# Shared-key attention on Trainium2: diagonal blocks masked by GpSimd on the exponentials in place of a mask product on TensorE

## The reference

```
q = (x @ Wq).reshape(B, T, 16, 16);  k = x @ Wk;  v = x @ Wv          # k, v: T x 16
scores = einsum('bihd,bjd->bhij', q, k) / sqrt(16)
scores = where(j <= i, scores, -inf)
out = einsum('bhij,bjd->bihd', softmax(scores), v) @ Wo + bo
```

## Time and profile before

| | us |
|---|---|
| median of 3 runs | 1820.72 (1815.22 to 1824.67) |
| the profiled execution | 1815.07 |
| its span | 1813.3 |
| TensorE busy | 1660.7 (92%) |
| VectorE busy | 1010.2 (56%) |
| ScalarE busy | 760.0 (42%) |
| GpSimd busy | 386.1 (21%) |
| score, mask and value products of the stage, busy | 205.3, 54.3, 150.0 |

### The profile page before, as it was taken

One profiled execution on the slowest core, in us unless ns is written; L12 is line 12 of the kernel. 1 busy time (PEld: TensorE's weight loads), 2 busy tenths in 40 slices (PEclk: granted clock), 3 DMA queues, 4 the chain that ended last, 5 costly groups with the idle time before them and its releaser, 6 DMA issues.

```text
span 1813.3 us, 25325 instructions
## 1 busy us (share of the span) xinstructions
PE 1660.7 (92%) x9852; PEld 985.2 (54%) x9852; DVE 1010.2 (56%) x1735; ACT 760.0 (42%) x1757; POOL 386.1 (21%) x457
## 2 busy tenths in 40 slices
PE   7999789999999999699997888968999999979998
PEld 4666444433333344445563555745677777764556
DVE  4665677777787753534435743325676666731222
ACT  3421346667667766131101121136666666632110
POOL 2321000001000000400000076514444443530000
PEclk9998889999999999699998999989999999999999
DMA  5000120000000002010000030000000020000000
GB/s 171 2 7 18 52 71 2 2 1 2 1 1 2 1 1 98 0 48 0 1 1 15 1 116 1 0 6 1 7 1 7 1 80 1 1 0 1 12 12 23
DMA packets 28360, 34.96 MB, mean 19 GB/s; under 512 B 5713, under 2 KB 24722, under 8 KB 27730
## 3 DMA queue, kind: packets, MB, share of 16 engines
q1 hardware_dynamic: 28242, 33.35, 5.8%
HBM read 23.74 MB, written 2.10 MB: 14 GB/s over the span
## 4 chain that ended last, share of the span: by engine, by line
PE 74%; DVE 13%; POOL 6%; issue 3%; ACT 3%; DMA 0%; SPq 0%; POOLq 0%; DVEq 0%; ACTq 0%
PE PS L1155 7%; PE PS L1142 6%; PE PS L1114 6%; PE PS L1396 6%; PE PS L1402 6%; PE PS L1417 5%; PE PS L2235 3%; DVE arena L1320 3%; PE PS L2224 2%; PE PS L1898 2%; PE PS L2202 2%; PE PS L1881 2%; PE PS L339 2%; POOL arena L2420 2%; PE PS L2177 2%
## 5 line engine op out<-in xcount | busy, mean ns | idle before, releaser
L1244 ACT ACTIVATE arena<-PS 128x512 f32<-128x512 f32 (+3 forms) x640 | 319.7, 534 | 174.3 <-PE PS L1142 77.7
L1320 DVE TENSOR_REDUCE arena<-PS 128x1 f32<-128x1024 f32 (+7 forms) x320 | 329.7, 1061 | 96.1 <-PE PS L1116 68.3
L1142 PE MATMUL PS<-arena 99*128 99x512 bf16 (+3 forms) x640 | 205.3, 352 | 1.4 <-ACT arena L1244 1.0
L1114 PE MATMUL PS<-arena 96*128 96x512 bf16 (+3 forms) x640 | 178.4, 357 | 18.3 <-DVE arena L1320 17.5
L190 POOL TENSOR_TENSOR rstd<-ve,mhalf 128x4 f32<-128x4 f32 x32 | 32.3, 1009 | 606.3 <-DVE ve L218 606.3
L1155 PE MATMUL PS<-arena 128*32 128x512 f32 (+3 forms) x1280 | 150.0, 541 | 2.8 <-ACT arena L1250 1.7
L185 ACT ACTIVATE XT<-PS 128x1024 f32<-128x1024 f32 x32 | 32.8, 1024 | 283.2 <-PE PS L178 283.2
L1142 PEld LDWEIGHTS PS<-arena 99*128 99x128 bf16 x640 | 60.5, 99 | 147.1 <-ACT arena L1244 115.5
L1396 PE MATMUL PS<-XT,arena 128*128 128x512 f32 x256 | 122.7, 602 | 5.6 <-DVE R L200 3.5
L2235 PE MATMUL PS<-arena 128*128 128x256 f32 x512 | 121.0, 379 | 2.0 <-DVE R L200 2.0
L1402 PE MATMUL PS<-XT,arena 128*128 128x512 f32 x256 | 120.3, 592 | 0.0
(11 more groups left out here) (241 smaller groups left out, 2832.4 us busy)
## 6 DMA issues: line engine op xcount, KB each, us to landing
arena<-arena SPq DMA_DIRECT2D x55, 128.0 KB, 2.4
XT<-in_L_attn_xT SPq DMA_DIRECT2D x4, 512.0 KB, 6.9
X<-in_L_attn_x SPq DMA_DIRECT2D x4, 512.0 KB, 9.2
arena<-in_L_attn_out_w SPq DMA_DIRECT2D x1, 2048.0 KB, 7.3
out<-X SPq DMA_DIRECT2D x4, 512.0 KB, 2.9
arena<-in_dmask SPq DMA_DIRECT2D x1, 1024.0 KB, 5.6
arena<-in_L_ffn_W_up SPq DMA_DIRECT2D x1, 1024.0 KB, 5.2
arena<-in_L_ffn_W_gate SPq DMA_DIRECT2D x1, 1024.0 KB, 7.3
```

Source lines behind the costliest of these rows:

```text
L1114: last = pe.matmul(flat[:, o:o + w], q, a.KS[0:SROWS, CH * kc:CH * kc + w], start=True, stop=kc < c)
L1142: last = pe.matmul(PS[:, b, lo:CH], a.KS[0:rows, P * j:P * (j + 1)], a.QS[0:rows, G1 * g + r, CH * c + lo:CH * (c + 1)], start=True, stop= ...
L1244: act.activation(a.PB[:, n % 3, r, lo:CH], PS[:, 4 + x % 3, lo:CH], ACT.Exp, scale=D0 ** -0.5).then_inc(a.e2, 1)
L1320: dve.tensor_reduce(dst, src, AX.X, ALU.max, negate=True).then_inc(a.m1, 1)
```

## The change

The mask of 0 and -1e30 in bf16 and the mask product on diagonal blocks are gone. The exponentials of a diagonal block are computed without a mask, and GpSimd then writes zero where the key is ahead of the query, in the triangle's 128 columns of all four heads, with one `affine_select` of 4 x 128 columns in place. A new semaphore `kept` counts these; `value` waits for it on diagonal blocks. `value(n)` runs in step n+1 in place of step n, and the copy of the sum, the sums, the spread and the inverse move one step with it. GpSimd's new work for block n+1 stands at step n, between `parts` and `spread`.

```diff
@@ Plan1.__init__ @@
-        self.steps = range(-AHEAD1, self.nb + 4)
+        self.steps = range(-AHEAD1, self.nb + 5)
@@
             if i < NI1 - 2:
-                self.den_at[self.first[i + 1] + 1] = i
-            self.rdt_at[self.first[i + 1] + 3] = i
-        self.den_at[self.nb] = NI1 - 2
-        self.den_at[self.nb + 1] = NI1 - 1
-        self.rdt_at[self.nb + 2] = self.rdt_at.pop(self.first[NI1 - 1] + 3)
+                self.den_at[self.first[i + 1] + 2] = i
+            self.rdt_at[self.first[i + 1] + 4] = i
+        self.den_at[self.nb + 1] = NI1 - 2
+        self.den_at[self.nb + 2] = NI1 - 1
+        self.rdt_at[self.nb + 3] = self.rdt_at.pop(self.first[NI1 - 1] + 4)
+        self.masked = {}
+        for n, (i, j, lo) in enumerate(self.blocks):
+            if j >= TPC * (i // 4):
+                self.masked[n] = len(self.masked)
@@ l1_set @@
-    pool.tensor_copy(a.mkb, a.mk).then_inc(a.z, 1)
@@ l1_pe: score @@
         last = pe.matmul(PS[:, b, lo:CH], a.KS[0:rows, P * j:P * (j + 1)], a.QS[0:rows, G1 * g + r, CH * c + lo:CH * (c + 1)],
-                         start=True, stop=j < TPC * c)
-        if j >= TPC * c:
-            last = pe.matmul(PS[:, b, lo:lo + P], k.identb[:, :], a.mkb, start=False, stop=True)
+                         start=True, stop=True)
@@ l1_pe: value @@
-        pe.wait_ge(a.e2, G1 * (n + 1))
+        if n in P1.masked:
+            pe.wait_ge(a.kept, P1.masked[n] + 1)
+        else:
+            pe.wait_ge(a.e2, G1 * (n + 1))
@@ l1_pe: the loop over steps @@
-        if 0 <= n < P1.nb:
-            value(n)
+        if 0 <= n - 1 < P1.nb:
+            value(n - 1)
@@ l1_act: the loop over steps @@
-        if n + 1 in P1.first[1:]:
-            values_out(P1.first.index(n + 1) - 1)
+        if n in P1.first[1:]:
+            values_out(P1.first.index(n) - 1)
@@ l1_pool @@
+    def keep(n):
+        lo = P1.blocks[n][2]
+        p = a.PB[:, n % 3, :, lo:lo + P]
+        pool.wait_ge(a.e2, G1 * (n + 1))
+        pool.affine_select(p, p, pattern=[[0, G1], [1, P]], compare_op=ALU.is_ge, fill=0.0, base=0, channel_multiplier=-1).then_inc(a.kept, 1)
+
     for n in P1.steps:
         if n in P1.mt_at:
             parts(P1.mt_at[n])
+        if n + 1 in P1.masked:
+            keep(n + 1)
         if n in P1.den_at:
             spread(P1.den_at[n])
```

More of the change, by code:

```diff
@@ L95, in constants @@
     c["mask_q"] = np.where(i[None, :] <= i[:, None], f(0), neg)
-    c["mask_k"] = np.where(i[:, None] <= i[None, :], f(0), neg)
+    c["keep_k"] = np.where(i[:, None] <= i[None, :], f(3e38), f(0))
     ahead = i[None, :] - i[:, None] % WIN3
@@ L920, in l1_alloc @@
     a.mqb = take([P, P], BF16)
-    a.mkb = take([P, P], BF16)
     a.denrow = take([P, G1])
@@ L940, in l1_alloc @@
     a.s2, a.e2, a.pv, a.ot = s("l1_scores"), s("l1_scores_bank_drained"), s("l1_values"), s("l1_values_evacuated")
+    a.kept = s("l1_probs_masked")
     a.rx, a.an, a.biased = s("l1_sum_inverse_spread"), s("l1_heads_normed"), s("l1_x_biased")
@@ L951, in l1_sp @@
                      (a.w[:, :, QK1:QKV1], w("L1_attn_Wv")), (a.bias, I["L1_attn_bo"].partition_broadcast(P)),
-                     (a.mq, I["mask_q"]), (a.mk, I["mask_k"]), (a.denrow, I["denrow"]), (a.krow, I["krow"])]:
+                     (a.mq, I["mask_q"]), (a.mk, I["keep_k"]), (a.denrow, I["denrow"]), (a.krow, I["krow"])]:
         sp.dma_start(dst, src).then_inc(a.ld, 16)
@@ L1096, in l1_pe @@
     pe.wait_ge(a.ev, VALUES1[2])
-    pe.wait_ge(a.z, 3)
+    pe.wait_ge(a.z, 2)
     def unit(u):
```

## The result

The changed kernel takes 1852.15 us (median of 4, 1851.79 to 1862.28) against 1817.97 us (median of 4, 1815.06 to 1824.67): a ratio of 1.0208 (95% interval 1.0178 to 1.0237), 34 us slower.

The account below looks back on a forecast made before the run. TensorE's stream of columns was taken to set the pace, VectorE close behind. The sum -11 - 2 + 40.2 - 4.5 + 0.3 = +23.0 us on 1815.07 gave 1838.1 profiled, 1844 as a median; range 1820 to 1872.

Parts of the forecast that it names:

- signs that were named: Changed profile: turn idle 2.5 to 3 us at 15 places, parts directly behind select, no mask products, granted clock 1.00.
- Mask products: TensorE in shared-key attention: 256 products at 0.06 us, 15 us, less a quarter: gain 11 us, bounds 8 and 15.
- Values later: Value products one step later: their wait for exponentials binds only in the last 25 blocks or so; gain 2 us, 0 to 4.
- The select's duration: GpSimd's zeroing of 4x128 columns per diagonal block, K: 1.04 us, bounds 0.61 and 1.41.
- The stalls: TensorE's 15 maxima turns wait for parts, queued behind the zeroing's wait for exponentials: 40.2 us, 33.8 to 45.8.
- the formula: Stall of one turn: exponential's end minus earlier turn start, plus select duration, 1.06 for parts, 0.2 for handovers; 3.0 us.
- What comes back: VectorE catches up during the stalls, so TensorE's short waits behind the turns go: 4.5 us, bounds 0 and 9.
- The end: End of the stage: zeroing and value products delay the last accumulator copy on ScalarE by 0.3 us.
- rival C: TensorE's granted clock falls in the turn stalls as well: 15 to 26 us more, 1853 to 1864 profiled; chance 0.13.
- forecast A: The maxima's turn stalls behind the diagonal zeroing: +8 to +39 us, 1829 to 1860 as a median; chance 0.64.
- Rival B: VectorE's owed maxima cover the turn stalls: 1808 median at full cover, faster under 0.9 us per turn; chance 0.15.
- Rival D: GpSimd's zeroing is much dearer than arithmetic: 2.93 us gives 1866 to 1872, 5 us about 1960; chance 0.08.

Follow-up runs that it names:

- values later: The kernel before with only values, copy of the sum, sums, spread and inverse one step later, mask product kept: 1815.74 us, ratio 0.9975, stage 491.9 us.
- filled turn: The changed kernel with 10 useless TensorE products ahead of the wait for parts at 15 turns: 1838.7 us, ratio 1.0101, stage 514.3 us.
- parts first: The changed kernel with GpSimd doing parts one step earlier, ahead of the zeroing: 1801.7 us, ratio 0.9901, stage 481.0 us.
- values not later: The changed kernel with parts ahead of the zeroing, but values in step n as in the kernel before: 1825.16 us, ratio 1.0055, stage 503.1 us.
- wait-only kernel: The kernel before with GpSimd waiting for the diagonal block's exponentials before parts at 15 turns, no zeroing: 1847.4 us, ratio 1.0166, stage 521.2 us.
- select twice: The changed kernel with the zeroing ahead of parts done twice, 15 selects more: 1873.25 us, ratio 1.0307, stage 556.1 us.

## Why the prediction was right, and where not

The direction, the place and the order of size were forecast: +23 us, and +34 between the medians, +39.4 in the stage. The main mechanism held as well: TensorE idles at 15 turns, released by the last operation of parts, which stands behind the select, and no value product waits for the select. One of the signs that were named didn't hold: the granted clock isn't 1.00 in the stage.

The stage lengths, taken as a chain from kernel to kernel, split the +39.4 us (that they add up is by construction): -0.8 (values later) - 10.8 (mask products) - 0.1 (the select itself) + 33.3 (stalls, filled turn against parts first) + 17.8 (the clock, changed against filled turn).

- **Mask products**, forecast -11: measured -10.8. The size of a mask product's slot and the quarter taken off are right together; no run separates them.
- **Values later**, forecast -2: -0.8 in the stage. The reading that the values' wait binds in the last 25 blocks or so only was wrong, as the run with values not later showed.
- **The select's duration**, taken at 1.04 us with bounds 0.61 and 1.41: 0.636. The nearest row was the copy with one operand, not the product with two. That is 6 us too much. The 768 ns of the Trainium skill, "GPSIMD Engine Reference", section "Elementwise — side-by-side cycle accounting", was nearer than my value, and still too high; by its price for data-dependent branching the select would have taken 5 us, and it didn't.
- **The stalls**, forecast 40.2, or 34.1 at the measured duration: TensorE waited 37.8 us. At item 14 the formula gives 0.71 + 0.64 + 1.06 + 0.2 = 2.6 us against 2.50. The term that was off is the difference between exponential and turn at items 3 to 8 (-0.62 to 0.19). I laid it to VectorE. It came in the main from the four products of `turn_inverse` ahead of these turns, and I wrote of the sums and inverses that "their distances stay": the change moved them behind the turn. The wait-only kernel, which keeps them in place, shows the shorter waits at these six items. With 0.7 us at all 15 turns the formula gives 39 us.
- **What comes back**, forecast 4.5: 37.8 us of waits against 33.3 us of stage leave 4.5. The figure is a difference between runs and agrees so well by luck, but the mechanism shows in part: TensorE's maxima products wait 12.2 us for VectorE in the stage of parts first, 9.0 us in the changed kernel. Against the kernel before, with its 8.2 us, none of these waits went: without the mask products they would have grown.
- **The end**, forecast 0.3 us. The last exponentials and the copy of the sum, to be held against the earlier trace rows:

```profile
772.59 0.45 ACT L1248 ACTIVATE arena<-PS 128x128 f32<-128x128 f32 x2 [0.65 <-PE PS L1145]
...
774.45 0.59 ACT L1254 ACTIVATE arena<-PS 128x512 f32<-128x512 f32 x1
```

  The copy starts 1.41 us behind the last exponential's end; before it was 1.47. At 0.64 us the select fits in: nothing.
- **The step that failed** is the one on the clock. I set it apart as rival C, 15 to 26 us with a chance of 0.13, and left it out of the sum. It happened: 17.8 us in the profiled executions' stages, 13.5 us between the medians. So what was measured is C by its mechanism, not the forecast A with its chance of 0.64. I had leaned on one place where 2.68 us of idleness left the clock at 1.00. One such row can't carry that: behind equal idle times of 2.50 us it fell at item 13 and stayed at item 14.

With the select at its real price and the clock left out, the forecast would have been +17, and the stage without the clock's part is 39.4 - 17.8 = 21.6 us longer; most of the difference is the stalls at items 3 to 8. The predicted 1844 was near the result partly because two errors, 6 us too much for the select and 14 to 18 too little for the clock, stood against each other. That is luck, and so is a part of the 8 us: the forecast started from a median of 1820.72 us for the kernel before, beside 1817.97 in the comparison, which brought it 3 us nearer. The difference was forecast 11 us too small.

Rival B (the stall is covered) had its point at 0.9 us of loss per turn: it was 33.3/15 = 2.2 without the clock. Rival D is excluded by the 636 ns.

What stays open: the medians of parts first and of values later only lie 19 and 5 us under the kernel before, while their stages are 11.7 and 0.8 us shorter. The kernel before scatters from 1808 to 1825 us and parts first from 1800 to 1806. What scatters is the part of the span that the change doesn't touch. Ahead of and behind the stage, first in the changed kernel and then in the one with the select twice:

```profile
0.00:240.90 240.90, 212.54 (x1920) 134.29 (x1921) 143.98 (x320) 64.16 (x152) 45.84 (x77) 0.91 0.17 50
773.00:1860.60 1087.60, 979.35 (x4605) 655.30 (x4603) 519.74 (x1019) 368.34 (x949) 307.93 (x299) 0.95 0.04 14
```

```profile
0.00:230.10 230.10, 200.53 (x1920) 126.96 (x1921) 143.79 (x320) 64.08 (x152) 45.77 (x77) 0.96 0.18 53
786.20:1867.90 1081.70, 973.31 (x4605) 651.41 (x4603) 518.52 (x1019) 368.03 (x949) 307.56 (x299) 0.96 0.04 14
```

The same work took 16.7 us longer there, with a granted clock of 0.91 and 0.95 in place of 0.96 and 0.96. This also places the 10 us by which the profiled execution of the changed kernel is above its other three: if the stage took them 532.1 us too, 1852.1 - 1.8 - 532.1 = 1318 us are left for the rest, as in parts first. The mean granted clock of the profiled execution is also the lowest of the four (0.948 against 0.954 to 0.956). That the stage was the same in all four isn't shown. Nor is it shown what sets the clock outside the stage, or why the kernel before has more of the long executions than parts first.

## What to carry to other kernels

When work goes to an idle engine, look at what stands behind it in that engine's queue, not at its share of busy time: a wait put ahead of a small operation that the critical engine needs turned a gain of 12 us of the stage into a loss of 39, and moving that operation ahead of the wait brought it back. Price the stall as the whole relay from the event to the waiting engine, look at which of the waiting engine's own work the change moves out of the gap, and count a fall of TensorE's clock as part of it. A move that gives nothing by itself (values one step later) can be what makes room for another edit, so judge room by the tightest instance, not by the first or the last.

## What the runs showed of the hardware

GpSimd's affine select of 4 x 128 float32 columns on 128 partitions, in place, took 634 to 644 ns, about as long as its copy of 512 columns (610 ns), with no dearer first one.

TensorE's granted clock fell from 1.00 to 0.50 at idle times that hardly differ from those at which it stayed. In each kernel with stalls the clock was still low at the first of the 15 turns. Of the other 14, with idle times of 2.5 us (one of 2.8) in the changed kernel, it fell in or just behind 11. In the wait-only kernel it fell at 4 of 8 with 1.9 us (one of 2.1) and at none of 6 with 0.9 to 1.5 us. With 3.2 us (one of 3.5) in the kernel with the select twice, it fell at all 14. Over the stage the mean fell with the length of the stall: 0.99, 0.96 and 0.93 for 1.9, 2.5 and 3.2 us. Useless work in the gap kept it at 1.00, but for one fall, and made the kernel 13.5 us faster. The Trainium skill, "TensorE: Matmul & The Clock Gate", section "What's actually happening", says that the low clock is the default and that activity lifts it; the filled turn agrees.
